# Two extra decay tiles in SBUF and later side work in a state-space stage, with other slots for two attention stages

## The reference, cut to what matters

```python
xz = x @ Win
xi, z = jnp.split(xz, 2, axis=-1)
xi = jax.nn.silu(_causal_dwconv(xi, convw, convb))
xdbc = xi @ Wx                       # dt_in, Bm, Cm
dt = jax.nn.softplus(dt_in @ Wdt + bdt)
A = -jnp.exp(Alog)
def step(h, inp):
    u_t, dt_t, B_t, C_t = inp
    dA = jnp.exp(dt_t[:, :, None] * A)
    h = dA * h + (dt_t * u_t)[:, :, None] * B_t[:, None, :]
    y = jnp.einsum('bds,bs->bd', h, C_t)
    return (h, y)
...
return y * jax.nn.silu(z) @ Wout
```

## Time and profile before

| | us |
|---|---|
| median of 3 runs | 5266.18 (5259.53 to 5272.27) |
| the profiled execution, its own time | 5254.81 |
| its span, first to last instruction | 5252.9 |

### The profile page before, as it was taken

How to read it: one execution, slowest core, us unless ns; L and a number is a source line. 1 busy time by engine, 2 the same in 40 slices (tenths; PEclk the granted TensorE clock), 3 DMA queues, 4 the chain that set the end, 5 groups by cost and what they waited for, 6 DMA issues and landing times. The chain is left out here.

```text
span 5252.9 us, 104514 instructions
## 1 busy us (share of the span) xinstructions
PE 4029.3 (77%) x29689; PEld 2335.5 (44%) x29692; DVE 4122.6 (78%) x8425; ACT 2797.7 (53%) x6477; POOL 2811.0 (54%) x3454
## 2 busy tenths in 40 slices
PE   5788787878878877877688868886283888789953
PEld 2333333333333333332466646665282666566632
DVE  5998888899888889987588877776145887767778
ACT  4555555555555555554577744444374554444435
POOL 5766666666666666765477742333543222233345
PEclk8988888898888888988799979996695999889965
DMA  2111110111111111100455535555114554365521
GB/s 87 69 39 67 71 71 37 71 71 67 38 71 71 39 69 71 71 35 39 94 108 105 105 78 118 113 116 159 51 53 119 108 108 99 75 129 116 111 56 32
DMA packets 320704, 420.70 MB, mean 80 GB/s; under 512 B 40512, under 2 KB 302224, under 8 KB 309648
## 3 DMA queue, kind: packets, MB, share of 16 engines
q1 hardware_dynamic: 316048, 408.35, 29.9%
q0 software_dynamic: 4352, 8.95, 0.5%
HBM read 307.65 MB, written 109.58 MB: 79 GB/s over the span
## 5 line engine op out<-in xcount | busy, mean ns | idle before, releaser
L1861 PE MATMUL bank<-m_h,ident 128*128 128x512 f32 x2048 | 1241.8, 701 | 423.8 <-DVE m_h L2127 371.7
L2228 POOL TENSOR_TENSOR m_h<-m_dtu,m_Bb 128x512 f32<-128x512 f32 x1024 | 1327.0, 1323 | 336.5 <-PE bank L1861 331.0
L2121 DVE TENSOR_TENSOR_SCAN m_h<-bank,m_h 128x512 f32<-128x512 f32 x1024 | 1246.3, 1217 | 192.8 <-ACT bank L2009 183.8
L2009 ACT ACTIVATE bank<-m_dt,m_A 128x512 f32<-128x512 f32 x1024 | 695.4, 688 | 748.0 <-DVE m_h L2121 662.0
L1861 PEld LDWEIGHTS bank<-m_h,ident 128*128 128x128 f32 x2048 | 390.7, 214 | 1081.4 <-DVE m_h L2127 847.1
L2127 DVE TENSOR_TENSOR m_h<-m_h,bank 128x512 f32<-128x512 f32 x1024 | 676.8, 661 | 6.7 <-PE bank L1854 6.7
L712 DVE TENSOR_REDUCE x_nm<-bank 128x4 f32<-128x308 f32 x512 | 239.3, 474 | 149.9 <-PE bank L370 144.3
L547 ACT ACTIVATE x_sm<-bank,x_nm 128x77 f32<-128x77 f32 x1024 | 318.2, 336 | 60.3 <-DVE x_nm L712 59.9
L537 ACT ACTIVATE f_pT<-bank 128x512 f32<-128x512 f32 x256 | 153.0, 598 | 239.9 <-PE bank L390 238.6
L1805 PE MATMUL bank<-m_xTp,m_wck 128*128 128x512 f32 x512 | 268.7, 630 | 12.1 <-ACT m_xTp L1923 12.1
L537 ACT ACTIVATE a_pT<-bank 128x512 f32<-128x512 f32 x256 | 153.4, 599 | 181.3 <-PE bank L390 180.3
(11 more groups left out here) (425 smaller groups left out, 9876.4 us busy)
## 6 DMA issues: line engine op xcount, KB each, us to landing
m_Bb<-m_B SPq DMA_DIRECT2D x32, 4096.0 KB, 12.2
x_Ks<-x_k_parts SPq DMA_DIRECT2D x64, 231.0 KB
x_q_parts<-x_qp SPq DMA_DIRECT2D x32, 384.0 KB, 3.9
x_Qs<-x_q_parts SPq DMA_DIRECT2D x32, 384.0 KB
f_Ks<-f_k_parts SPq DMA_DIRECT2D x32, 384.0 KB
a_Ks<-a_k_parts SPq DMA_DIRECT2D x32, 384.0 KB
x_xp<-x_stage SPq DMA_DIRECT2D x32, 256.0 KB
...
```

The costliest lines, as they stand in the source:

```text
L1861: pe.matmul(banks[4 + c], ident[:], h[:, k % RING, :], start=(s == 0), stop=(s == NS - 1)).then_inc(s_ya.sem, 1)
L2009: act.activation(decays[k % AHEAD], dt[:, d, c, :], ACT.Exp, scale=A[:, d, c, s:s + 1]).then_inc(s_dA.sem, 1)
L2121: v.tensor_tensor_scan(h[:, k % RING, :], decays[k % AHEAD], h[:, k % RING, :], 0.0, ALU.mult, ALU.add).then_inc(s_h.sem, 1)
L2228: pool.tensor_tensor(h[:, k % RING, :], dtu[:, d, c, :], Bb[:, d, s, :], ALU.mult).then_inc(s_dB.sem, 1)
```

## The change

1. The state-space stage gets a tile `spare_decays` in SBUF, [128, 2, 512]. In slots 26 and 27 of a forward unit and 25 and 26 of a backward unit (IN_SBUF) the decay is written there, and the scan reads it there, in place of bank k % 2. Each decay now waits for the last scan that read its own buffer (`last_reader`): a decay in SBUF waits for the unit before, and the two decays in PSUM behind them wait for scan k-4.
2. `exp` is cut in two side steps, `exp` and `one`, each with its slot.
3. Side work stands in other slots. Forward, ACT: dt0 19 to 20, dt1 23 to 21, exp 23 to 22 (one 23), log 25 to 27, yT 23 to 28, move 26 to 29, m0 29 to 30, m1 27 to 31; PE: yT 21, 22 to 22, 23, m0 24 to 27, m1 27 to 28. Backward, ACT: f 1 to 4, f_norm 6 to 9, c1 10 to 11, f_out 13 to 15, xd 16 to 17, one 23, log 24 to 26, o 24 to 27, move 26 to 28, o_norm 29 to 31; PE: xT before the first half of f in slot 0, dt0, dt1 16, 17 to 17, 18; DVE: f_stats 2 to 5, f_affine 8 to 10, e 22 to 23, o_stats 25 to 27, dtu 28 to 30. POOL's table is the same.
4. Norm-first attention: norm steps, x, q and k in other slots. RMS attention: x, qt, kt and v in other slots. The stages with a context keep theirs.

```diff
-    norm_at = (-12, -11, -8, -7)
+    norm_at = (-12, -8, -4, -3)
     if rms:
-        slot = {"x": -11, "qt": -10, "kt": -9, "qn": -2, "kn": -1, "v": 3}
+        slot = {"x": -12, "qt": -11, "kt": -8, "qn": -2, "kn": -1, "v": 0}
...
     elif ln is not None:
-        slot, later = {"x": -6, "q": -5, "k": -4, "v": 3}, {"v": 3, "high": 1, "middle": 2}
+        slot, later = {"x": -2, "q": -1, "k": 0, "v": 3}, {"v": 3, "high": 1, "middle": 2}
...
-             {0: ["f:0", "xT"], 1: ["f:1", "c1:0"], 2: ["c0:0"], 3: ["c1:1", "c1:2"], 6: ["c0:1"], 7: ["c1:3"], 8:
...
+             {0: ["xT", "f:0"], 1: ["f:1", "c1:0"], 2: ["c0:0"], 3: ["c1:1", "c1:2"], 6: ["c0:1"], 7: ["c1:3"], 8:
...
+    IN_SBUF = ((26, 27), (25, 26))
...
-        decays = (banks[0], banks[1])
+        spare = sb("spare_decays", [P, 2, GT])
+
+        def decay_buffer(d, k):
+
+            return spare[:, k % 2, :] if k in IN_SBUF[d] else banks[k % 2]
+
+        def last_reader(d, k):
+
+            back = 2
+            while ((k - back) % SL in IN_SBUF[(d + (k - back) // SL) % 2]) != (k in IN_SBUF[d]):
+                back += 2
+            return k - back
+
...
                     act.activation(flat(cc[:]), flat(cc[:]), ACT.Exp, scale=-1.0).then_inc(s_z.sem, 1)
+                if what == "one":
                     act.wait_ge(s_z.sem, s_z.at(n + 1))
                     act.activation(flat(tu[:]), flat(cc[:]), ACT.Identity, bias=one[:]).then_inc(s_w1.sem, 1)
...
-                act.wait_ge(s_h.sem, s_h.at(n, k + 1 - AHEAD))
-                act.activation(decays[k % AHEAD], dt[:, d, c, :], ACT.Exp, scale=A[:, d, c, s:s + 1]).then_inc(s_dA.sem, 1)
+                act.wait_ge(s_h.sem, s_h.at(n, last_reader(d, k) + 1))
+                act.activation(decay_buffer(d, k), dt[:, d, c, :], ACT.Exp, scale=A[:, d, c, s:s + 1]).then_inc(s_dA.sem, 1)
...
-                v.tensor_tensor_scan(h[:, k % RING, :], decays[k % AHEAD], h[:, k % RING, :], 0.0, ALU.mult, ALU.add).then_inc(s_h.sem, 1)
+                v.tensor_tensor_scan(h[:, k % RING, :], decay_buffer(d, k), h[:, k % RING, :], 0.0, ALU.mult, ALU.add).then_inc(s_h.sem, 1)
```

More of the change, by code:

```diff
@@ L1543, in mamba @@
     LAG = 2
-    AHEAD = 2
     TURNS = NG // 2
@@ L2031, in turn @@
                         unit(2 * i + l, l, d)
-            for what in ("xT", "c1", "c0", "z0", "z1", "xd", "move", "dt0", "dt1", "exp", "log"):
+            for what in ("xT", "c1", "c0", "z0", "z1", "xd", "move", "dt0", "dt1", "exp", "one", "log"):
                 prep(use_first, 0, 0, what)
```

18 lines of the change are left out of this document (10 added, 8 removed).

## The result

| | us |
|---|---|
| before, median of 4 runs beside it | 5262.85 (5259.41 to 5272.27) |
| changed kernel, median of 4 runs | 5128.59 (5109.34 to 5137.26) |
| ratio | 0.9737, interval 0.9706 to 0.9768 |
| the profiled execution's span | 5107.5 (before 5252.9) |

The kernel became faster by 2.6%, some 138 us by the ratio. The forecast was 60. The time lies in the range, and close to the number of rival B; the profile shows that rival B is not what happened. The profiled execution is the fastest of the four, so its 145 us are a little more than the change is worth.

A forecast was written before the change was run, and what follows sets the result against it. DVE was taken to set the pace, stopped by 183.8 us of waits for ACT's decays. State-space −45, norm-first attention −15 and RMS attention 0 gave −60: 5206 us against 5266.2, range 5115 to 5250.

The forecast's parts named there:

- rival B: State-space stage: scans with both inputs in SBUF run undisturbed; −123 and −15 in attention give 5128 us; chance 0.22.
- waits for ACT in the forward unit: Forward tail: three scans' waits for log and m1, 6.0 us together, are covered; −6.0 us a pair.
- forward SBUF scans: Forward slots 26 and 27: each scan loses the rest of a POOL op, 0.9 and 1.85; +2.8 us a pair.
- backward head, slots 0 and 1: Start of the backward unit: xT earlier by 1.5 us, f's copy out of slot 1 for 0.62; −2.1 us a pair.
- backward slots 24 to 31: Backward tail, us a pair: log wait −1.3, new POOL wait at scan 27 +2.3, lo −1.1, SBUF scans +2.4.
- The lock: State-space tails: SBUF scans and POOL ops hold each other up; +2.8 forward and +2.4 backward, us a pair.
- The state-space term: State-space stage: waits removed, less new waits and longer scans, −3.0 us a pair, times 15 pairs: −45 us.
- The attention term: Norm-first attention −15 us, half of PE's waits of up to 30; RMS attention 0, with 11 to either side.
- C: Forward tail: ACT's lead of decays doesn't build up, 2.8 us a pair stay, +42: 5248 us; chance 0.14.
- D: Four SBUF scans: lock costs more than the decays gave, from 9.4 us a pair; slower, 5301 us; chance 0.07.
- E: Freed time is taken by PE's adds at the backward head and POOL's queue in the tails: 5266 us; chance 0.05.

The follow-up runs named there:

- change_again: The changed kernel run once more, unaltered, in another group; 0.9765 (0.9752 to 0.9778) against the kernel before.
- m1_only: The kernel before with m0 and m1 of the forward tail moved on PE and ACT as in the change; 0.9905 (0.9880 to 0.9929), 50 us.
- mamba_only: The changed kernel without the diff's attention lines, so only the state-space stage changed; 0.9844 (0.9817 to 0.9871), 82 us.
- duo: The kernel before with xT first, f's chain moved at the backward head, and m0 and m1 moved in the forward tail; 0.9822 (0.9808 to 0.9835), 93 us.
- swap: The kernel before with xT ahead of the first half of f in PE's slot 0 of a backward unit; 0.9999 (0.9986 to 1.0012).
- dt_31: The changed kernel with POOL's dt of a backward unit in slot 31 in place of 26; 0.9758 (0.9742 to 0.9773) against the kernel before.

## Why the prediction was wrong

The direction was right and the stages gained where it said. The sum was less than half of the change, by two terms of about equal weight: 37 us in the state-space stage and 39 in the attention. For a pair, from the mean lengths of the 32 slots of a unit (scan start to scan start) over the 14 inner units of each direction, the changed kernel against the kernel before, in its two profiles:

| term | forecast | after | change_again |
|---|---|---|---|
| waits for ACT in the forward unit | −6.0 | −5.9 | −5.9 |
| forward SBUF scans | +2.8 | +2.3 | +2.3 |
| backward head, slots 0 and 1 | −2.1 | −3.1 | −2.5 |
| f_stats and f_affine, moved | 0 | −0.6 | −0.6 |
| slot 13 (`u`) | 0 | +0.7 | +0.7 |
| backward slots 24 to 31 | +2.3 | +1.5 | +1.5 |
| all other slots | 0 | 0 | −0.6 |
| a pair | −3.0 | −5.1 | −5.1 |

**What bounds the kernel** was right: DVE, with the waits for decays at three places, and `m1` apart from `log` (`m1_only`, 50 us).

**The lock** was right, and it was the term with the largest doubt: forecast +2.8 and +2.4 by the rows of L2064 and L2228; the 64 scans took 161.6 us by the form of their group, 2526 ns each, where 64 from a bank take 78. The forecast left open whether scans would start late or last longer, but counted them as late; they start in time and last longer. The Trainium skill ("SBUF — State Buffer", "Who interferes with whom") says that whichever starts first has the shared ports for the whole instruction; the trace agrees, and adds that a scan then needs another 1.08 us of its own.

**Rival B** gives 5128, the number measured, by the opposite mechanism. Its condition, that all SBUF scans start at once and last 1.2 us, is refuted by the changed kernel's profiles, where 62 of 64 meet a POOL op. A right total is no evidence for a theory.

**The state-space term was mis-sized**, −45 for what measured 82 (68 to 96). Over 15 pairs the table gives 76 and the lead-in and lead-out of the stage the rest (the profile of `mamba_only` has 4.1 a pair in place of 5.1). The runs say where the miss lies. The head was forecast at 31 and measured 35, `m1` at 57 (3.78 x 15) and measured 50, both together at 88 and measured 93. All the rest, `log` behind the SBUF decays with the lock and POOL's `dt`, was forecast to cost 43 us more, and cost some 11 (`mamba_only` against `duo`, with some 16 to either side). So the step that failed is the price of the two tails. Backward, the wait at slot 27, forecast as 4.7 with the lock in it, came out as 0.59 and 3.3 of longer scans: the forecast laid the held instructions end to end at their full lengths, and each is 0.1 to 0.2 us shorter behind its release. Forward, the scans cost 2.3 in place of 2.8, and the waits for `log` alone were 2.6 us in the mean where the unit read had 2.2. `lo` was forecast by one case of 1.75 us; its mean before was 1.35.

At the head the forecast took 1.5 for `xT`, and at one clock it is 1.2 to 1.3. That the clock itself would differ between the two kernels' profiles was not in the sum: the slots 0 of both units together are 2.0 us shorter in either profile of the changed kernel, and the swap explains 1.3 of it.

**The attention term was mis-sized**, −15 for what measured 54. The larger failed step is the RMS attention: "nothing in the rows says which way: 0". A term was put at nothing because its sign was unknown, and it was worth 28 us by the means of the profiles, beyond the 11 allowed to either side. Why the new slots help there no run shows. In the norm-first attention, worth 24, the step "Only PE's waits can be won" failed: 23 of the 30.1 us of waits did go, but PE's own busy time fell by 17 us as well, at a granted clock of 0.97 for 0.94, and the forecast had held it fixed.

**The range** reached 5115 and held the time only since B's and the attention's bounds were in it; by the mechanism forecast, that was luck. The chance of 0.86 for faster was sound.

**Rivals C, D and E** did not happen: no scan of a forward tail waits for ACT, the two locks cost 5.5 us a pair in longer scans, under the 9.4 from which D decides, and the gain did not shrink to nothing. What E describes did happen in two experiments, `swap` and, for the most part, `dt_31`.
